# The high part of y1 taken as a second gated product out of the PSUM bank

## What is computed

```python
def ffn(x):                       # weights are ternary, D_HID = 512
    h = silu(tlin(x, w1_w, w1_s)) * tlin(x, w2_w, w2_s)      # the gated layer
    h = gelu(tlin(h, h1_w, h1_s))
    h = gelu(tlin(h, h2_w, h2_s))
    return tlin(h, w3_w, w3_s)    # tlin(x, w, s) = (x @ w.T) * s
def attn(x):                      # h_t = tanh(x_t B + h_(t-1) A.T), a scan over the tokens
    return (hs @ C) @ W_out.T + b_out
x = x + 0.5 * ffn(layernorm(x))
x = x + attn(layernorm(x))
x = x + 0.5 * ffn(layernorm(x))
```

## Time and profile before

| | us |
|---|---|
| median of 3 runs | 440.8 |
| lowest, highest | 440.43, 441.01 |
| the profiled execution | 441.55 |
| its span, first to last instruction | 439.7 |

### The profile page before, as it was taken

One profiled execution on the slowest core, in us unless ns is written; L12 is line 12 of the kernel. 1 busy time (PEld: TensorE's weight loads), 2 busy tenths in 40 slices (PEclk: granted clock), 3 DMA queues, 4 the chain that ended last, 5 costly groups with the idle time before them and its releaser, 6 DMA issues.

```text
span 439.7 us, 6738 instructions
## 1 busy us (share of the span) xinstructions
PE 398.6 (91%) x1896; PEld 313.0 (71%) x1896; DVE 325.2 (74%) x688; ACT 234.4 (53%) x462; POOL 163.0 (37%) x152
## 2 busy tenths in 40 slices
PE   0448999999999999999999999999999999999981
PEld 0235777787878878787787878778787878777760
DVE  2467889899898989856869775968869595978511
ACT  2417646465664646456554556546464555646450
POOL 3105525244454524244433333534323343524220
PEclk9999999999999999999999999999999999999996
DMA  7900000000000000000101000010100001010001
GB/s 223 430 12 0 1 25 0 26 1 5 20 2 25 0 24 0 24 1 0 49 0 50 1 24 25 0 50 0 48 0 32 16 0 48 0 50 0 26 1 33
DMA packets 6048, 13.98 MB, mean 32 GB/s; under 512 B 1280, under 2 KB 1664, under 8 KB 5760
## 3 DMA queue, kind: packets, MB, share of 16 engines
q1 hardware_dynamic: 6016, 13.60, 8.3%
HBM read 7.31 MB, written 2.10 MB: 21 GB/s over the span
## 4 chain that ended last, share of the span: by engine, by line
PE 59%; DVE 16%; issue 14%; ACT 4%; POOL 3%; DMA 1%; SPq 0%; DVEq 0%; ACTq 0%; POOLq 0%
PE F L228 47%; PE FR L228 5%; DVE y L601 3%; DVE u L591 3%; DVE h_wide L645 2%; DVE y_lo L618 2%; PE SC L347 2%; DVE y_hi L608 2%; ACT y_hi L869 2%; PE MI L353 2%; POOL y_lo L1042 1%; DVE xnt_f L580 1%; DMA w_raw<-in_w2T 1%; PE MI L237 1%; PE FR L257 1%
## 5 line engine op out<-in xcount | busy, mean ns | idle before, releaser
L228 PE MATMUL F<-y_hi,w_hi 128*128 128x512 f32 x512 | 214.9, 420 | 7.4 <-DVE y_lo L618 4.0
L228 PE MATMUL F<-y_lo,w_hi 128*128 128x512 f32 x512 | 202.6, 396 | 0.0
L1042 POOL TENSOR_TENSOR y_lo<-y,y_hi 128x512 fp32r<-128x512 f32 x96 | 131.7, 1385 | 135.4 <-ACT y_hi L869 64.4
L866 ACT ACTIVATE y<-F,sc 128x512 f32<-128x512 f32 x112 | 77.1, 688 | 120.3 <-PE F L228 120.2
L228 PEld LDWEIGHTS F<-y_hi,w_hi 128*128 128x128 f32 x512 | 96.6, 189 | 34.7 <-issue 9.0
L228 PEld LDWEIGHTS F<-y_lo,w_hi 128*128 128x128 f32 x512 | 96.6, 189 | 19.8 <-issue 1.9
L618 DVE TENSOR_TENSOR y_lo<-y,y_hi 128x512 fp32r<-128x512 f32 x96 | 85.0, 896 | 34.3 <-ACT y_hi L869 32.1
L869 ACT ACTIVATE y_hi<-F,sc 128x512 fp32r<-128x512 f32 x112 | 76.7, 685 | 0.0
L848 ACT ACTIVATE th<-F,s1h 128x512 f32<-128x512 f32 x64 | 44.3, 692 | 33.0 <-PE F L228 20.1
L228 PE MATMUL F<-xn_hi,w_hi 128*128 128x512 f32 x127 | 54.3, 428 | 3.0 <-DVE xn_lo L586 2.9
L228 PE MATMUL F<-xn_lo,w_hi 128*128 128x512 f32 x127 | 51.2, 403 | 0.0
(11 more groups left out here) (86 smaller groups left out, 312.2 us busy)
## 6 DMA issues: line engine op xcount, KB each, us to landing
x_all<-in_xT SPq DMA_DIRECT2D x1, 2048.0 KB, 15.7
x_all<-x1c SPq DMA_DIRECT2D x8, 256.0 KB, 2.3
x_all<-lnin SPq DMA_DIRECT2D x8, 256.0 KB, 2.3
out<-outb SPq DMA_DIRECT2D x8, 256.0 KB, 2.1
x_all<-in_xtok SPq DMA_DIRECT2D x1, 1792.0 KB, 11.5
w_raw<-in_h1T SPq DMA_DIRECT2D x2, 512.0 KB, 6.0
w_raw<-in_h2T SPq DMA_DIRECT2D x2, 512.0 KB, 7.6
x_all<-in_xtok SPq DMA_DIRECT2D x1, 256.0 KB, 2.8
```

The lines of the kernel that those rows point to most:

```text
L228: mm = nc.tensor.matmul(out, wtile(w, layer, k, m), y, start=first and i == 0, stop=last and i == len(pairs) - 1)
L866: nc.scalar.activation(y23[:, m, :], bankt[:, :], ACT.Gelu, scale=s)
L1042: pool.tensor_tensor(y_lo[:, k, :], y[:, k, :], y_hi[:, k, :].bitcast(F32), ALU.subtract).then_inc(out_sem, 1)
```

## The change

In `gated` VectorE now takes the gated product twice from the bank and u: first to y1_hi, with the rounding on the way out, then to y1 in full precision. The cast of y1 (`y1_high`) is gone. Since y1_hi is announced ahead of y1, whoever needs both waits for y1 as well: GpSimd's low parts of blocks 0 to 2 and VectorE's of block 3 (`y1_low`). All 60 casts of groups 1 to 15 are replaced; group 0 is left as it was.

```diff
             def gated(g, m, late=False):
                 dve.wait_ge(u_r, 4 * g + m + 1)
+                bankt = (B1_LATE if late else B1)[m][1]
+                if not late:
+                    wait(dve, l2_mm, 4 * g)
+                    nc.vector.scalar_tensor_tensor(out=y1_hi[:, m, :], in0=bankt[:, :], scalar=s12h[:, m:m + 1],
+                                                   in1=u[:, m % 2, :], op0=ALU.mult, op1=ALU.mult).then_inc(y1_hi_r, 1)
                 if m < KT - 1:
                     wait(dve, y1_lo_pool, (KT - 1) * (g - 1) + m + 1)
                 else:
                     wait(dve, y1_lo_dve, g)
-                nc.vector.scalar_tensor_tensor(out=y1[:, m, :], in0=(B1_LATE if late else B1)[m][1][:, :],
-                                               scalar=s12h[:, m:m + 1], in1=u[:, m % 2, :],
-                                               op0=ALU.mult, op1=ALU.mult).then_inc(y1_r, 1)
-
-            def y1_high(g, m):
-                dve.wait_ge(y1_r, 4 * g + m + 1)
-                wait(dve, l2_mm, 4 * g)
-                nc.vector.tensor_copy(y1_hi[:, m, :], y1[:, m, :]).then_inc(y1_hi_r, 1)
+                nc.vector.scalar_tensor_tensor(out=y1[:, m, :], in0=bankt[:, :], scalar=s12h[:, m:m + 1],
+                                               in1=u[:, m % 2, :], op0=ALU.mult, op1=ALU.mult).then_inc(y1_r, 1)
...
+            def y1_low(g):
+                dve.wait_ge(y1_r, 4 * g + KT)
+                low(g, KT - 1, y1_hi_r, y1, y1_hi, y1_lo, y1_lo_dve)
...
             def layer1(g, ms=range(KT - 1)):
                 for m in ms:
+                    pool.wait_ge(y1_r, 4 * g + m + 1)
                     low(g, m, y1_hi_r, 4, y1, y1_hi, y1_lo, y1_lo_pool, (l2_mm, 4 * g))
```

More of the change, by code:

```diff
@@ L612, in layer1 @@
                 gated(g, m, late)
-                if not late:
-                    y1_high(g, m)
             def low(g, k, hi_r, y, y_hi, y_lo, out_sem):
@@ L618, in low @@
                 nc.vector.tensor_tensor(y_lo[:, k, :], y[:, k, :], y_hi[:, k, :].bitcast(F32), ALU.subtract).then_inc(out_sem, 1)
+            def y1_low(g):
+                dve.wait_ge(y1_r, 4 * g + KT)
+                low(g, KT - 1, y1_hi_r, y1, y1_hi, y1_lo, y1_lo_dve)
             def last_gated(g):
                 gated(g, KT - 1)
-                y1_high(g, KT - 1)
-                low(g, KT - 1, y1_hi_r, y1, y1_hi, y1_lo, y1_lo_dve)
+                y1_low(g)
             def layer4(phase, g, c):
@@ L687, in early_turn @@
                 low(g, 3, y3_hi_r, y23, y3_hi, y3_lo, y3_lo_dve)
-                low(g + 1, KT - 1, y1_hi_r, y1, y1_hi, y1_lo, y1_lo_dve)
+                y1_low(g + 1)
                 if mid is not None:
@@ L786, in _ @@
                 layer1(0, m, late=True)
-            low(0, KT - 1, y1_hi_r, y1, y1_hi, y1_lo, y1_lo_dve)
+            y1_low(0)
             early_turn(0, None)
@@ L810, in round_ @@
                         layer1(gb + CHUNKS, m, late=True)
-                    low(gb + CHUNKS, KT - 1, y1_hi_r, y1, y1_hi, y1_lo, y1_lo_dve)
+                    y1_low(gb + CHUNKS)
                     turn(0, gb + CHUNKS, (gb + 2, 2))
```

## The result

The changed kernel takes 444.4 us (median of 4 runs, 443.9 to 445.1) against 440.6 us before (4 runs): 1.0088 times as long, 95% interval 1.0071 to 1.0106, so 3.8 us slower. The forecast was 442.2, slower, with a range of 439.9 to 444.9. The direction was right and the time lies in the range, near its upper end; the loss is 2.7 times the 1.4 us that the sum gave, and outside the sum's own range of 441.2 to 443.4.

A forecast was written before the change was run, and what follows sets the result against it. TensorE's matmul stream bounds the kernel. Turns 1 to 6 -0.8, 7 and 8 +0.2, 10 +0.1, 11 to 13 +0.9, 14 +0.44, 15 +0.6 make +1.4 us: median 440.8 to 442.2, range 439.9 to 444.9.

The forecast's parts named there:

- the sum: Net change over turns 1 to 15 at places (a), (b) and (c): +1.4 us, giving 442.2 us; chance 0.45.
- The instruction: Product replacing the cast on VectorE: 0.75 us each, rounding free, none longer, 0.66 us ahead of the product to y.
- VectorE's busy time: VectorE over the whole kernel: grows by 10 us, to 335 us, on an engine with slack.
- Place (a), the bank: TensorE's wait for y1 of m=0 before layer 1's block 2 reuses its bank: 4.2 us gross of new waiting.
- Place (b), the collision: Last y3_lo before layer 4's last product: without the cast, one GpSimd operation less delays VectorE; turns 1 to 6 net -0.8 us.
- Place (c): y1_lo of m=3 before the next layer 2, longer serial path: +0.3 us in turns 11 to 13, +0.44 in 14.
- my sign for the tail: Matmul behind y1_lo of m=3: the tail term is wrong if it has no wait in turns 11 to 14.
- port first: Rival at the port VectorE shares with GpSimd: y_lo waits for a second subtraction of 1.2 us; 444.6 us, chance 0.17.
- my sign for the order at the port: y_lo right behind y of m=2: about 1.1 us expected; port order wrong if it takes 1.8 us or more.

The follow-up runs named there:

- before_later: Kernel before, but GpSimd's low part of y1 in block 2 waits for VectorE's y3_lo of block 2, nothing left out: ratio 0.9919, 437.3 us.
- m2_twice: Against the kernel before, only block 2 takes the product twice, the other blocks keep product and cast: ratio 0.9985, 1.0 us faster.
- after_short: Changed kernel with GpSimd's low parts of y1 in blocks 1 and 2 cut to 8 of 512 columns: ratio 1.0013 to the kernel before.
- before_short: Kernel before with GpSimd's low parts of y1 in blocks 1 and 2 cut to 8 of 512 columns from group 1 on: ratio 0.9919.

## Why the prediction was right in direction and short by 2.4 us

**The instruction.** Right: 0.75 us each, no collision, 0.66 us ahead of the next product (130.38 to 131.05 in turn 4, 0.67). **VectorE's busy time.** Wrong, 324.4 and not 335: I added the product and took off neither the overlap of neighbours, which I used for the path, nor what y_lo loses of its collisions, on which I counted two paragraphs further down.

**Place (a), the bank.** The mechanism held, and the ten turns are the ones I named, with the small ones where I had them. The term was over-sized: 4.2 against 3.1. In the seven turns with 0.47 us of slack it is 0.15 and not 0.3. Two sizes made the difference: y_hi starts 0.71 to 0.73 us after u (129.67 to 130.38), where the old product in the loops started 0.83 after it, and a release takes 0.06 us here (y ends at 46.97 + 0.74 = 47.71 in turn 1 and the matmul starts at 47.77), where I had taken 0.10. The restart of the stream, 0.06 to 0.08 us in turns 1 and 15 and 0.02 to 0.03 in turns 4 and 11, went the other way and was not in my sum:

```profile
46.97 0.74 DVE L606 SCALAR_TENSOR_TENSOR y<-F,s12h,u 128x512 f32<-128x512 f32 x1
```

```profile
47.77 0.50 PE L228 MATMUL F<-xn_hi,w_hi 128*128 128x512 f32 x1 [0.42 <-DVE y L606]
```

**Place (b), the collision: the step that failed.** The prediction said that with the cast gone VectorE "issues the first y_lo (at about 305.45) while GpSimd's first operation still runs", and that u of block 3 comes half a us earlier. It followed VectorE's queue and the port, and left out what y_lo reads: ScalarE's y_hi of layer 3, block by block. In turn 11 of before that y_hi ended at 305.64, and y_lo started at 305.69; the cast that stood before y_lo had delayed it by next to nothing. In turn 4 of before it had delayed the first y_lo by about 0.25 us (ScalarE done at 125.32, y_lo at 125.61), but the second y_lo did not inherit that, since it waited for ScalarE's next y_hi, which ended at 127.49. Before, turn 4, ScalarE and VectorE:

```profile
126.81 0.68 ACT L869 ACTIVATE y_hi<-F,sc 128x512 fp32r<-128x512 f32 x1
```

```profile
127.53 1.56 DVE L618 TENSOR_TENSOR y_lo<-y,y_hi 128x512 fp32r<-128x512 f32 x1
```

So most of the relief fell into idle time of VectorE (in front of y_lo it grew by 12 us), and the tail of block 3 kept VectorE last at layer 4. The collision worth removing was that of the second y_lo, and before_later removes it alone. Turns 1 to 6 were to gain 0.8 us and lost 2.2: this one step is 3 us of error, and the over-sized bank hides a part of it. m2_twice measures the relief alone, 1.0 us in the whole kernel.

**Place (c).** The size fits the trace, the place only in part. Attention gives back 0.17 to 0.19 us per turn, as I had it. But in turns 10 to 13 TensorE loses it again at the transposes of lnin, for which I had no wait: they start 0.33 us after lnin ends in both kernels (311.82 to 312.15 in turn 11 before, 313.58 to 313.91 after), which I read as a wait for lnin, though the profile names no releaser. The matmul behind y1_lo of m=3, my sign for the tail, has next to no wait in turns 11 to 13 (0.24 us behind the one in front of it, where 0.23 is usual) and 0.08 us in turn 14; it adds 0.04 us per turn. By that sign the tail was all but wrong here. Net 0.17 to 0.24 where I had 0.3 to 0.44, for the bank term that fed it was double. Turn 15: 0.58 against 0.6.

**The rivals.** The time is that of "port first" (444.6). Its order did occur, in turns 1 and 5 and, because of ScalarE, in 10 to 14, and there my sign for the order at the port (1.8 us or more; 1.1 was expected) went against me in two turns. In turn 1 y_lo and GpSimd's second operation both started at 52.18 us, and y_lo lost (two of them in one line, 1.84 and 1.68 us):

```profile
52.18 3.55 DVE L615 TENSOR_TENSOR y_lo<-y,y_hi 128x512 fp32r<-128x512 f32 x2 [0.32 <-ACT y_hi L869]
```

But the order did not set the price: turn 5 lost what turns 4 and 6 lost, and in the pair after_short and before_short the distance without the collisions is the same 3.9 us. The price of the rival was near the truth because it, too, amounted to striking the credit of place (b). So it is partly luck that the time lies in the range: the sum's own range ended at 443.4, and the upper end of 444.9 came from this rival.

## What to carry to other kernels

Relief on an engine is worth what the next operation can use: before an operation is moved forward, look up when each of its inputs is ready, not only when its engine and its port are free. An instruction that replaces a cheap one but reads a PSUM bank holds that bank longer; the price is set by the slack between the last read and the matmul that reuses the bank (0.05 to 0.12 us in three turns, 0.47 in seven), and most of it can be had back by using the new form only in the blocks whose bank nobody waits for. Where two engines share a port, a late start of the operation that nobody waits for (3.5 us here) can be worth more than a faster instruction.

## What the runs showed of the hardware

A product of one PSUM and one SBUF operand is written rounded at the price of the unrounded one (0.751 us in the changed kernel, 0.751 for the unrounded one before), and of the 60 the 27 that ran while GpSimd subtracted took 0.754 us at most. Two independent products of VectorE start 0.66 us apart although each is listed with 0.75 (130.38 and 131.05, 311.08 and 311.74). The time from the end of a VectorE operation to the start of the matmul that waits for it was 0.05 to 0.06 us at the bank and 0.15 us behind y_lo (0.33 behind lnin, if that is a wait at all); I have not found what makes the difference, and no run here was made for it. An operation with two SBUF operands that takes 0.69 us alone takes 1.78 when GpSimd's subtraction is in front of it, and it did so in all eight of h_wide. When both asked at nearly the same time, it went either way: a y_lo at 126.11 against GpSimd's 126.13 took 0.69 us (and GpSimd 1.82), one at 151.44 against 151.45 took 1.85 (and GpSimd 1.29). In the traces of the five kernels in which block 2 is taken twice and nothing else is moved or left out, the two started less than 25 ns apart in 35 turns, and VectorE went first in 30 of them.
